# Mixing the softmax maps ahead of the maxima, with GpSimd's operations in pieces, a doubled rotation buffer and weight loads on ScalarE's queue

## What is computed

```
q, k, v = x @ Wq, x @ Wk, x @ Wv            # 16 query heads, 4 key/value heads
q1, q2, k1, k2 = rope of the halves of q, k  # rotation: turned = x*cos + swapped(x)*sin
a1 = softmax(q1 @ k1.T * scale + causal mask)
a2 = softmax(q2 @ k2.T * scale + causal mask)
out = (a1 - lam * a2) @ v
out = group_norm(out, per batch and head) * gn_w + gn_b
x = layer_norm(x + 0.8 * out @ Wo)
x = layer_norm(x + top2_experts(x))
```

## Time and profile before

| | us |
|---|---|
| median of 3 runs (1975.13 to 1981.24) | 1976.45 |
| the profiled execution, its own time | 1986.36 |
| its span from the first to the last instruction | 1984.5 |
| PE busy | 1683.6 (85%) |
| DVE busy | 1393.5 (70%) |
| ACT busy | 1167.2 (59%) |
| GpSimd busy | 579.9 (29%) |

### The profile page before, as it was taken

How to read it: one execution, slowest core, us unless ns; L and a number is a source line. 1 busy time by engine, 2 the same in 40 slices (tenths; PEclk the granted TensorE clock), 3 DMA queues, 4 the chain that set the end, 5 groups by cost and what they waited for, 6 DMA issues and landing times. The chain is left out here.

```text
span 1984.5 us, 35122 instructions
## 1 busy us (share of the span) xinstructions
PE 1683.6 (85%) x9718; PEld 1254.2 (63%) x9719; DVE 1393.5 (70%) x3225; ACT 1167.2 (59%) x3388; POOL 579.9 (29%) x471
## 2 busy tenths in 40 slices
PE   4878898898899899999889889874999999999600
PEld 3556566656666655656656655534999999999500
DVE  4898988988988988988988898634333333333376
ACT  2777878878788788787887887732222222222133
POOL 0322312522432432332341251014423343000174
PEclk8999999999999999999999999876999999999855
DMA  8764755665574584574484575024433343333286
GB/s 276 226 175 124 196 148 139 204 178 149 170 203 117 165 228 112 147 220 131 141 233 128 147 223 147 22 92 166 162 118 118 126 156 119 119 92 103 75 268 207
DMA packets 141439, 311.17 MB, mean 157 GB/s; under 512 B 16608, under 2 KB 19296, under 8 KB 140160
## 3 DMA queue, kind: packets, MB, share of 16 engines
q1 hardware_dynamic: 111264, 231.64, 41.3%
q0 software_dynamic: 15072, 50.74, 7.7%
q10 hardware_dynamic: 14976, 27.27, 3.6%
HBM read 207.87 MB, written 101.71 MB: 156 GB/s over the span
## 5 line engine op out<-in xcount | busy, mean ns | idle before, releaser
L853 ACT ACTIVATE expd<-S,neg_max 128x128 f32<-128x128 f32 (+3 forms) x1024 | 531.5, 536 | 146.4 <-DVE neg_max L1039 145.2
L1039 DVE TENSOR_REDUCE neg_max<-S 128x2 f32<-128x768 f32 (+3 forms) x384 | 399.3, 1040 | 142.7 <-PE S L661 138.8
L1070 DVE SCALAR_TENSOR_TENSOR mixed<-expd,rho 128x384 f32<-128x384 f32 (+3 forms) x512 | 340.6, 685 | 0.0
L657 PE MATMUL S<-kT,qT 128*128 128x256 f32 (+2 forms) x1024 | 277.1, 373 | 25.2 <-DMA qT<-parts_rows 18.7
L865 ACT ACTIVATE probsT<-PTp 128x512 f32<-128x512 f32 (+2 forms) x384 | 205.5, 535 | 91.9 <-PE PTp L672 88.5
L672 PE MATMUL PTp<-ident,mixed 128*128 128x128 f32 x1280 | 212.6, 281 | 53.8 <-DVE mixed L1070 49.5
L1526 ACT ACTIVATE xT_hi<-xTp 128x512 fp32r<-128x512 f32 x72 | 43.1, 599 | 358.8 <-DVE yo L1707 352.9
L657 PEld LDWEIGHTS S<-kT,qT 128*128 128x128 f32 x1024 | 162.7, 193 | 127.8 <-issue 81.7
L719 PE MATMUL tail<-wo,ctxT 128*128 128x512 f32 x464 | 218.7, 594 | 0.0
L853 ACT ACTIVATION_READ_ACCUMULATOR expd<-S,neg_max 128x1 f32 x1024 | 216.2, 211 | 0.0
L552 POOL TENSOR_TENSOR swapped<-swapped,rope_t 128x512 f32<-128x512 f32 x77 | 98.8, 1283 | 384.7 <-DVE swapped L1032 384.7
(11 more groups left out here) (245 smaller groups left out, 3675.8 us busy)
## 6 DMA issues: line engine op xcount, KB each, us to landing
qT<-parts_rows SPq DMA_DIRECT2D x256, 256.0 KB, 4.4
parts_rows<-parts SPq DMA_DIRECT2D x160, 256.0 KB, 2.5
wqk<-wqk_split SPq DMA_DIRECT2D x75, 512.0 KB, 6.1
xin<-expert_in_rows SPq DMA_DIRECT2D x72, 256.0 KB, 2.9
expert_out_rows<-yo ACTq DMA_DIRECT2D x72, 256.0 KB, 3.2
kT<-parts_rows SPq DMA_DIRECT2D x64, 256.0 KB, 4.5
x<-in_x SPq DMA_DIRECT2D x8, 1024.0 KB, 7.2
x_rows<-x SPq DMA_DIRECT2D x8, 1024.0 KB, 7.7
```

What stands on the lines that cost most here:

```text
L657: nc.tensor.matmul(S[s % 2][:, k * slot:k * slot + w], qT[kv % 2][:, 2 * h + c, i * P:(i + 1) * P], kT[kv][:, c, 0:w], start=(k % per_bank ...
L853: ex = nc.scalar.activation(expd[s % 3][:, k * slot:k * slot + w], S[s % 2][:, k * slot:k * slot + w], ACT.Exp, bias=neg_max[s % 3][:, k:k ...
L1039: nc.vector.tensor_reduce(neg_max[s % 3][:, 0:k], v, AX, ALU.max, negate=True).then_inc(max_ready, 1)
L1070: ins = nc.vector.scalar_tensor_tensor(out=mixed[sl % 3][:, a * 256:a * 256 + w], in0=e2, scalar=rr[:, i, h:h + 1], in1=e1, op0=ALU.mult, ...
```

## The change

- `mix` of unit s-2 stands at the head of DVE's step, ahead of `maxes`.
- `ratios` is one tensor_scalar for each head (one tensor read, the factor and the reciprocal as scalars of a partition) in place of one scalar_tensor_tensor, which reads two tensors.
- The three GpSimd operations of a group are each issued as four of 128 columns (`PIECES`).
- `turned` is doubled. `rotate` of group n waits for the low part of group n-2 and for the rope of group n-1, in place of the low part of group n-1.
- The weights of the next group but one are loaded by ACT, one step after the last chunk of the group that leaves the buffer; SP keeps the spreads and no longer waits for a projection, but for the one ahead of the load of the next batch's x.
- On PE the tail tasks other than "oproj" stand at the end of the step, behind `values`.

```diff
+PIECES = [slice(o, o + T // 4) for o in range(0, T, T // 4)]
...
-        turned = sb("turned", [P, T])
+        turned = [sb(f"turned{r}", [P, T]) for r in range(2)]
...
-                    sp.wait_ge(prep_full, fill_no(b, idx))
-                    apart(sp)
-                    if not (last and idx + 2 >= THIS_BATCH):
-                        sp.dma_start(wqk[idx % 2][:].bitcast(F32), wsplit_dram[:, (idx + 2) % NGRP]).then_inc(w_in[idx % 2], 16)
...
-                nc.gpsimd.tensor_tensor(swapped[:], swapped[:], sin, ALU.mult).then_inc(rope_step, 1)
+                for o in PIECES:
+                    ins = nc.gpsimd.tensor_tensor(swapped[:, o], swapped[:, o], sin[:, o], ALU.mult)
+                ins.then_inc(rope_step, 1)
...
                     if not first:
                         for task in TAIL_PE.get(s, []):
-                            tail_task(b - 1, 1 - par, task)
+                            if task[0] == "oproj":
+                                tail_task(b - 1, 1 - par, task)
...
+                    if not first:
+                        for task in TAIL_PE.get(s, []):
+                            if task[0] != "oproj":
+                                tail_task(b - 1, 1 - par, task)
...
+            def next_weights(b, first, idx):
+
+                act.wait_ge(prep_full, fill_no(b, idx))
+                if first and idx == 0:
+                    act.wait_ge(wsplit_stored, 16 * 8)
+                nc.scalar.dma_start(wqk[idx % 2][:].bitcast(F32), wsplit_dram[:, (idx + 2) % NGRP]).then_inc(w_in[idx % 2], 16)
...
                 dve.wait_ge(prep_full, fill)
-                at_least(dve, lo_done, n)
+                at_least(dve, lo_done, n - 1)
+                apart(dve)
+                at_least(dve, rope_done, n)
...
-                nc.vector.scalar_tensor_tensor(out=rr[:, i, h0:h0 + nh], in0=L[:, i, 0, h0:h0 + nh],
-                                               scalar=neg_lam[:, 0:1], in1=Q[:, i, 1, h0:h0 + nh],
-                                               op0=ALU.mult, op1=ALU.mult).then_inc(rho_step, 1)
+                for h in heads:
+                    ins = nc.vector.tensor_scalar(rr[:, i, h:h + 1], L[:, i, 0, h:h + 1], Q[:, i, 1, h:h + 1],
+                                                  neg_lam[:, 0:1], ALU.mult, ALU.mult)
+                ins.then_inc(rho_step, 1)
...
+                    if lagged(b, s, 2, first):
+                        mix(*lagged(b, s, 2, first))
                     maxes(s, u)
                     if lagged(b, s, 1, first):
                         inverse_sums(*lagged(b, s, 1, first))
-                    if lagged(b, s, 2, first):
-                        mix(*lagged(b, s, 2, first))
```

More of the change, by code:

```diff
@@ L337, in attention_block @@
         PLAN_COLS = 2 * E + E * E + MT * E
-        plan, zrow = expd[0][:, 0:PLAN_COLS], turned
+        plan, zrow = expd[0][:, 0:PLAN_COLS], turned[0]
         block = ctx.enter_context(nc.Block())
@@ L503, in body @@
                         continue
-                    sp.wait_ge(prep_full, fill_no(b, idx))
-                    apart(sp)
-                    if not (last and idx + 2 >= THIS_BATCH):
-                        sp.dma_start(wqk[idx % 2][:].bitcast(F32), wsplit_dram[:, (idx + 2) % NGRP]).then_inc(w_in[idx % 2], 16)
                     if idx == 6 and not last:
+                        sp.wait_ge(prep_full, fill_no(b, idx))
+                        apart(sp)
                         sp.dma_start(x_next[:], xT_d[:, b + 1]).then_inc(xT_in, 16)
@@ L546, in take_vals, with rope @@
                 nc.gpsimd.tensor_copy(vals[kv][:], vnext[:, :, kv * HD:(kv + 1) * HD]).then_inc(vals_ready, 1)
-            def rope(n, fill, kind):
+            def rope(n, r2, fill):
                 sin = rope_t[:, 1, :]
                 pool.wait_ge(prep_out, fill)
-                nc.gpsimd.tensor_tensor(swapped[:], swapped[:], sin, ALU.mult).then_inc(rope_step, 1)
+                for o in PIECES:
+                    ins = nc.gpsimd.tensor_tensor(swapped[:, o], swapped[:, o], sin[:, o], ALU.mult)
+                ins.then_inc(rope_step, 1)
                 pool.wait_ge(rope_step, n + 1)
-                nc.gpsimd.tensor_tensor(turned[:], turned[:], swapped[:], ALU.add).then_inc(rope_done, 1)
+                for o in PIECES:
+                    ins = nc.gpsimd.tensor_tensor(turned[r2][:, o], turned[r2][:, o], swapped[:, o], ALU.add)
+                ins.then_inc(rope_done, 1)
             def low_part(n, r2):
                 pool.wait_ge(hi_done, n + 1)
-                nc.gpsimd.tensor_tensor(parts[r2][:, 1, :], turned[:], parts[r2][:, 0, :].bitcast(F32),
-                                        ALU.subtract).then_inc(lo_done, 1)
+                for o in PIECES:
+                    ins = nc.gpsimd.tensor_tensor(parts[r2][:, 1, o], turned[r2][:, o], parts[r2][:, 0, o].bitcast(F32), ALU.subtract)
+                ins.then_inc(lo_done, 1)
             idx = sb("idx", [P, NT, TOPK], U32)
@@ L585, in body @@
                         if SEQ[idx][0] != "v":
-                            rope(group_no(b, idx), fill_no(b, idx), SEQ[idx][0])
+                            rope(group_no(b, idx), half(b, idx), fill_no(b, idx))
                     if not first and not second:
@@ L949, in high_part @@
                 act.wait_ge(rope_done, n + 1)
-                nc.scalar.activation(parts[r2][:, 0, :], turned[:], ACT.Copy).then_inc(hi_done, 1)
+                nc.scalar.activation(parts[r2][:, 0, :], turned[r2][:], ACT.Copy).then_inc(hi_done, 1)
             mine = {8: [("gsq", 0)], 10: [("gn", 0)], DONE + 1: [("ln", 0)], DONE + 11: [("wt", 0)]}
@@ L974, in body @@
                             high_part(group_no(b, idx), half(b, idx), stack_total(b, idx) - GROUP_COUNT)
+                    for idx in fills(s, last, 1):
+                        if SEQ[idx][0] != "v" and not (last and idx + 2 >= THIS_BATCH):
+                            next_weights(b, first, idx)
                     for idx in fills(s, last, 0):
@@ L1025, in _, with rotate @@
         def _(dve):
-            def rotate(n, fill, kind):
+            def rotate(n, r2, fill):
                 dve.wait_ge(prep_full, fill)
-                at_least(dve, lo_done, n)
+                at_least(dve, lo_done, n - 1)
+                apart(dve)
+                at_least(dve, rope_done, n)
+                apart(dve)
                 cos = rope_t[:, 0, :]
-                nc.vector.tensor_tensor(turned[:], prep[:], cos, ALU.mult)
+                nc.vector.tensor_tensor(turned[r2][:], prep[:], cos, ALU.mult)
                 nc.vector.stream_shuffle(swapped[:], prep[:], [i ^ 1 for i in range(32)]).then_inc(prep_out, 1)
@@ L1255, in body @@
                         if SEQ[idx][0] != "v":
-                            rotate(group_no(b, idx), fill_no(b, idx), SEQ[idx][0])
+                            rotate(group_no(b, idx), half(b, idx), fill_no(b, idx))
                     if X_ROUND < s <= X_ROUND + DC and not last:
@@ L1408, in _ @@
             for i in range(LEAD - 2):
-                rotate(i, i + 1, HEAD[i][0])
+                rotate(i, i % 2, i + 1)
                 dve.wait_ge(prep_out, i + 1)
@@ L1413, in _ @@
                 dve.wait_ge(rope_step, i + 1)
-                nc.vector.tensor_tensor(turned[:], turned[:], swapped[:], ALU.add).then_inc(rope_done, 1)
+                nc.vector.tensor_tensor(turned[i % 2][:], turned[i % 2][:], swapped[:], ALU.add).then_inc(rope_done, 1)
                 low_w(3 + i)
                 dve.wait_ge(hi_done, i + 1)
-                nc.vector.tensor_tensor(parts[i % 2][:, 1, :], turned[:], parts[i % 2][:, 0, :].bitcast(F32),
+                nc.vector.tensor_tensor(parts[i % 2][:, 1, :], turned[i % 2][:], parts[i % 2][:, 0, :].bitcast(F32),
                                         ALU.subtract).then_inc(lo_done, 1)
```

## The result

The changed kernel takes 1992.43 us (median of 6 runs, 1987.83 to 2001.87), the kernel before in the same comparison 1976.45: a ratio of 1.0079, 95% interval 1.006 to 1.0099. It is slower by 16 us where I forecast 25 us faster. The profiled execution has 1990.06 us around a span of 1988.2.

The account below looks back on a forecast made before the run. No single engine was held to bound attention: the limit changes by stretch, with VectorE and GpSimd locking each other out. Terms gave -2.4 us a middle batch, -25.5 with the first two batches: 1951 us, range 1922 to 1980.

Parts of the forecast that it names:

- stretch 1: Steps 0 to 11 of an attention batch, 35.6 us in the fifth batch, where VectorE is busy 34.3.
- term 2: Steps 0 to 11: GpSimd's pieces delay group 1 of q's low part and step 12; +1.7 us a batch (-3.5 to +5).
- stretch 2: Steps 12 to 16 of an attention batch, 17.0 us in the fifth batch, where ScalarE is busy 16.2.
- term 3: Steps 12 to 16: the mix fills VectorE's idle gap before the maxima and a mix wait goes; -2.2 us a batch.
- stretch 3: Steps 17 to 35 of an attention batch, 64.2 us in the fifth batch, with PE busy all the time.
- term 4: Steps 17 to 35: PE stays busy, VectorE has room and two score banks give exponentials a spare step; 0 us.
- stretch 4: Steps 36 to 47 of an attention batch, 41.1 us in the fifth, where ScalarE and PE wait for each other.
- term 5: Steps 36 to 47: values go ahead of "xT" and mix waits shrink; -1.9 us a batch, ends 0 and -4.
- Term 1: VectorE's stalls beside GpSimd: pieces give VectorE back some 10 to 12 of 14.7 us a batch.
- rival (c): GpSimd keeps the lock from piece to piece, so VectorE stays out; -0.3 us a batch, 1974 us, chance 0.12.
- Rival (b): Pieces take 2.3 us or more an operation and the read-back shares with weights; +3.7 a batch, 1988 us, chance 0.13.

Follow-up runs that it names:

- e8: The kernel before with only the mix of a unit two back moved ahead of the step's maxima: 1.0149, 2003.6 us.
- e4: The changed kernel with the mix back behind the step's maxima and reciprocals: 0.9989, 1975.1 us.
- e2: The changed kernel with the weights' loads back on SP's queue: 0.998, 1973.9 us.
- e7: The kernel before with only the weights' loads moved to ScalarE's queue: 1.0114, 1999.0 us.
- e10: The kernel before with one weights' load in eight, group 4's, on ScalarE's queue: 1.0108, 1998.8 us.
- e6: The kernel before with only GpSimd's three operations of a group in four pieces each: 0.9963, 1968.8 us.
- e1: The changed kernel with GpSimd's three operations of a group whole again: 1.0213, 2019.9 us.
- e11: e5 with the old ratios by scalar_tensor_tensor, one instruction a unit: 0.9917, 1962.8 us.
- e12: The kernel before with only the tail's tasks other than the output projection behind the values: 0.9948, 1967.8 us.
- e5: The changed kernel with the weights' loads back on SP's queue and the mixes behind the maxima: 0.9933, 1962.5 us.

## Why the prediction was wrong, by its own steps

| step | predicted, us a batch | measured |
|---|---|---|
| stretch 1 (term 2) | +1.7 (-3.5 to +5) | +3.1 |
| stretch 2 (term 3) | -2.2 | +0.4 |
| stretch 3 (term 4) | 0 | +0.3 |
| stretch 4 (term 5) | -1.9 | -1.5 |
| a middle batch | -2.4 | +2.3 |
| second batch | -5.1 | +1.9 |
| first batch | -6 | -4.6 |

(The measured stretches and the middle batch are means over the second to the seventh batch; without the second the middle batch still has +2.3.)

**The step that failed most: the place of the mix.** Terms 3 and 5 took gains from a mix that fills VectorE's gap ahead of the maxima, and term 4 said that two banks give the exponentials a step to spare. Alone the move costs 29 us (e8); with the other parts around it, 18 (e4 against the changed kernel). The waits for a mix that I priced did go; I didn't price what waits for the maxima. The cover that term 4 named (up to 0.6 us a step if it were gone) mostly held in stretch 3, which grows by 0.3 us in the changed kernel and, with whole operations, by 1.1 us over 19 steps (e8); in the stretches where TensorE is not the limit it did not. No rival of mine had this mechanism, though the earlier trace rows show ScalarE waiting for the maxima: what I called its cover was its place in the loop.

**The load.** I saw the collision, gave it up to 2.2 us by shares of bandwidth, and took none of it, "since the load should be mostly ahead". In the changed kernel it was mostly ahead, and still took 18 us in all (e2): I had left out the stores, which it meets first, and the clock after a longer wait. Alone it costs 21 to 23 us (e7, e10), some 3 a batch: 1.5 to 1.7 us for the read-back; the rest I put down to the clock and what follows, and no run separates them. In the second batch load and read-back were issued together, and that batch, to which I gave 5.1 us for its missing scatters, lost 1.9 us. The low part of group 1 was late as in my sum (+1.75 forecast, +1.1 measured in the fifth batch, +1.4 in the mean); but the 10.8 us behind it, which I took as fixed (11.0 in the mean), became 11.9. The stretch's end, +3.1, I had at +1.7.

**Term 1, stalls.** The pieces' price was right: 1.65 forecast, 1.7 alone, 2.1 with mixes in between. They do let VectorE in (rival (c) is out), and alone gain 7 us (e6). VectorE's gain was under half of the forecast, 4.5 of 10 to 12 us a batch: mixes 43.1 to 37.0, ratios 14.45 to 16.0 where I had 10.1. I had overlooked that the new code issues one ratio a head, 64 a batch, and that the form costs 0.27 us; that it does not stall was right: its longest is 277 ns even in the kernel with whole operations (e1), where 118 of the 512 began while one of GpSimd's ran. The rule that I weighed (the Trainium skill, VectorE: DVE Perf Modes, What auto-detection actually checks) gives conditions for the mode with both port pairs; these rows bear no sign of the mode, and no run here tells at which size it would set in. The form made no difference to the time (e11).

**Term 5** was right for the tail's tasks, and undersized: the forecast gave them -1.0 (-0.7, and -1.8 where the clock dips), e12 measures -1.6 a batch (-1.1 and -2.7) and 10 us in all. The other -1.0, for two waits for a mix, was nothing: stretch 4 is as short with the mix behind (e4).

**Rival (b)** had the sign and nearly the time (1988) but did not come about as it says, though a price for the load was right in kind: the operations of that stretch took 1.7 to 2.2 us, under the 2.3 that it asked for, the read-back grew by 0.3 us and not by 2.2, and stretch 1 stayed at +3.1, under the +4.1 from which it outweighs the other terms. That its time is near is luck.

**The sum in runs,** each step against the one ahead of it: pieces -7 us (e6); the tail's tasks, doubled turned and ratios -6 (e5); mixes ahead +9 (e2); the load's queue +20 (changed), all by their ratios. In another order the last two read +11 for the load (e4) and +18 for the mixes. That what they share is the wait for group 1 of q is argued, not shown.

**Left open:** how the load's and the mix's shares in stretch 1 come about in detail; why e12's 10 us and e6's 7 add up to 16 (e11) while e5 has 13, which is within the intervals; and the doubled turned, which wasn't run alone.

## What to carry to other kernels

An engine's idle time ahead of an instruction is slack only if nobody waits for that instruction: before work is moved into it, list who stands behind, and price their wait at the length of what is moved in, stalls included. A bulk load must be placed in time, not on a queue: look at what urgent transfers, stores too, are under way at its new issue. And when an edit has six parts, the good ones (here the tail's tasks behind the values, and the pieces) hide behind the bad: run them apart.

## What the runs showed of the hardware

A wait of TensorE costs more than its length where the clock falls behind it. Ahead of the scores of step 12 the clock stayed at 1.00 after 1.50 us of idling (before, fourth batch); it was 0.54 for 3.7 us after 2.19 us (before, third batch) and after 3.05 us (e10), and 0.55 for 5.5 us after 5.05 us (changed, fifth batch). The length alone does not tell: of two waits of 2.01 us at "xT" in step 39 of the kernel before, one was followed by a clock of 1.00 (fourth batch, 634 to 637), the other by 0.64 (fifth batch, 790.3 to 795).

A tensor_scalar on one column took 262 to 277 ns in 512 instructions, beside GpSimd or not, while the scalar_tensor_tensor on one or two columns took 203 at least and 1249 at most.
